# The start of a state-space kernel: normalize, transpose and split ahead of the branch, splits on GpSimd, gates ahead of the mixing matrix

## The reference, cut to what matters

```
xn  = layernorm(x)                       # x: 8 batches x 512 tokens x 512
xz  = xn @ W_in.T;  x_ssm, z = split(xz) # 1024 + 1024 columns
xc  = silu(causal_conv4(x_ssm) + conv_b)
p   = xc @ W_x.T                         # 16 B, 16 C, one dt
dt  = softplus(p[..., -1] + mean(dt_bias));  A = -exp(A_log)
h_t = exp(A dt_t) h_{t-1} + dt_t B_t x_t;  y_t = C_t . h_t
s   = ((y + D xc) * silu(z)) @ out_W.T
g   = silu(ffn_with_attention(xn))
out = x + s * g
```

## Time and profile before

| | |
|---|---|
| three runs | 2586.34 us median (2586.32 to 2586.46) |
| the profiled execution | 2587.55 us, its span 2585.4 us |
| PE busy | 2487.2 us, 96% of the span |
| DVE busy | 1382.6 us, 53% |
| ACT busy | 1059.4 us, 41% |
| POOL busy | 439.8 us, 17% |
| mean granted TensorE clock | 0.989 |
| first 110 us: PE busy | 70.12 us |
| 110 to 182 us: PE busy | 71.76 us |
| batch 1: last add into PFM (L1161) | 194.81 to 195.50 us |
| batch 1: turned(1, 0) on PE starts | 199.78 us |

### The profile page before, as it was taken

The page is one execution under the profiler, slowest core; times in us unless marked ns, Lnnn a source line. Parts: engine busy times, 40 slices in busy tenths (PEclk is TensorE's granted clock), DMA queues, the critical chain, the costliest instruction groups (busy, mean ns, idle before and its releaser), DMA issues.

```text
span 2585.4 us, 38397 instructions
## 1 busy us (share of the span) xinstructions
PE 2487.2 (96%) x14359; PEld 2002.0 (77%) x14359; DVE 1382.6 (53%) x2876; ACT 1059.4 (41%) x1764; POOL 439.8 (17%) x407
## 2 busy tenths in 40 slices
PE   5899999999999899999999899999999999999998
PEld 4678778778788677777777678888888788888887
DVE  6666667567565578888888852212213422222223
ACT  4444444444544367777777641111112211111111
POOL 0000000000000234444443610000000202222222
PEclk8999999999999999999999999999999999999999
DMA  4000000000003577666566411111113312222212
GB/s 140 17 17 17 33 17 17 33 1 33 17 1 103 162 213 207 188 183 185 155 183 184 153 58 49 49 49 49 49 49 110 135 41 97 96 98 95 97 66 82
DMA packets 106972, 228.12 MB, mean 88 GB/s; under 512 B 14976, under 2 KB 15488, under 8 KB 100624
## 3 DMA queue, kind: packets, MB, share of 16 engines
q1 hardware_dynamic: 106528, 225.34, 27.2%
q10 hardware_dynamic: 256, 0.26, 0.0%
HBM read 149.77 MB, written 75.50 MB: 87 GB/s over the span
## 4 chain that ended last, share of the span: by engine, by line
PE 86%; DVE 6%; ACT 3%; issue 3%; DMA 2%; SPq 0%; POOL 0%; DVEq 0%; POOLq 0%; ACTq 0%
PE PS L72 13%; PE PS L74 13%; PE PS L73 13%; PE PS L2122 4%; PE PS L2123 4%; PE PS L2124 4%; PE PS L1622 3%; PE PS L1641 3%; PE PS L1599 2%; PE PS L708 2%; PE PS L707 2%; PE PS L709 2%; PE PS L1601 2%; PE PS L1600 2%; PE PS L693 1%
## 5 line engine op out<-in xcount | busy, mean ns | idle before, releaser
L2191 DVE TENSOR_TENSOR SG<-SG,PS 128x512 f32<-128x512 f32 x124 | 85.2, 687 | 645.4 <-PE PS L74 643.5
L72 PE MATMUL PS<-FH,GU 128*128 128x512 f32 x992 | 387.4, 390 | 1.4 <-DVE DW L2182 1.4
L74 PE MATMUL PS<-FH,GU 128*128 128x512 f32 x992 | 388.3, 391 | 0.0
L73 PE MATMUL PS<-FL,GU 128*128 128x512 f32 x992 | 387.5, 391 | 0.0
L1807 DVE CUSTOM_DVE_ANT_0 PS<-PS,MK 128x512 f32<-128x512 f32 (+3 forms) x512 | 243.8, 504 | 95.2 <-PE PS L1622 94.0
L2161 ACT ACTIVATE SG<-PS 128x512 f32<-128x512 f32 x124 | 74.0, 597 | 467.3 <-PE PS L2098 467.3
L1744 ACT ACTIVATE PF<-PS 128x512 f32<-128x512 f32 (+1 forms) x384 | 199.6, 526 | 84.8 <-PE PS L1643 82.8
L2227 POOL TENSOR_SCALAR XN<-XT,MEAN,RSTD 128x512 f32<-128x512 f32 x32 | 69.5, 2171 | 943.6 <-DMA M<-m_scratch 943.6
L2164 ACT CAST GH<-SG 128x512 fp32r<-128x512 f32 x124 | 76.9, 620 | 351.7 <-DVE SG L2191 351.7
L72 PE MATMUL PS<-XH,WH 128*128 128x512 f32 x512 | 211.1, 412 | 9.9 <-DVE XL L977 9.9
L72 PEld LDWEIGHTS PS<-FH,GU 128*128 128x128 f32 x992 | 186.4, 188 | 42.5 <-issue 1.8
(11 more groups left out here) (296 smaller groups left out, 5306.1 us busy)
## 6 DMA issues: line engine op xcount, KB each, us to landing
qk_scratch<-QT SPq DMA_DIRECT2D x128, 256.0 KB, 4.6
QS<-qk_scratch SPq DMA_DIRECT2D x96, 256.0 KB, 4.0
KS<-qk_scratch SPq DMA_DIRECT2D x96, 256.0 KB, 3.9
FH<-rh_scratch SPq DMA_DIRECT2D x16, 1024.0 KB, 5.7
FL<-rl_scratch SPq DMA_DIRECT2D x16, 1024.0 KB, 7.9
XF<-in_x_dram SPq DMA_DIRECT2D x32, 256.0 KB, 3.8
s_scratch<-ZS SPq DMA_DIRECT2D x8, 1024.0 KB, 4.4
rh_scratch<-RH SPq DMA_DIRECT2D x8, 1024.0 KB, 9.6
```

What stands on the lines that cost most here:

```text
L72: pe.matmul(o, lh(k), xh(k), start=open_ and k == 0, stop=False, skip_group_check=True)
L73: pe.matmul(o, lh(k), xl(k), start=False, stop=False, skip_group_check=True)
L74: last = pe.matmul(o, ll(k), xh(k), start=False, stop=close and k == nk - 1, skip_group_check=True)
```

## The change

- The first code, ahead of the branch, takes over much of the start. DVE: after step 4 of fast_deviations it makes four constants (which waits for the loads of idn and UM, c_ld 32), normalizes the four tiles of XF, runs step 5, makes the other constants, then split_lo(0) and the four lowered, and last RMS. PE: the 16 transposes of normed. ACT: the exponential of A_log, split_hi(0), normed_hi, split_hi(1). Each engine branches only after that.
- split_lo(1), (2) and (3) and the two subtractions for OL go from DVE to POOL, at the head of its fast path, ahead of RC (L1201) of batch 0.
- out_hi(0) and out_hi(4) on ACT move into the conv loop, at d = 4 and d = 5.
- gate(0, 0) on PE moves ahead of rows(0, 6), into bank 2 (bank_g); it waits for s_cv 9.
- For all batches: gate(b, 2) stands ahead of decays, gate(b, 3) ahead of factors_turned, gate(b, 4) ahead of off_diagonal, and none between off_diagonal and gate(b, 5). On ACT gated(b, 2) stands ahead of the two exponentials, and the later ones follow.
- Counts of semaphores follow; the general path, not run here, waits for what the first code started.

```diff
@@ first_vector
-            for step in range(8):
+            for step in range(5):
                 fast_deviations(dve, 0, step)
+            block_constants(dve, 0)
+            for k in range(4):
+                fast_normalized(dve, 0, k)
+            fast_deviations(dve, 0, 5)
+            block_constants(dve, 1)
+            dve.wait_ge(c_ld, 32)
+            split_lo(dve, 0)
+            for k in range(4):
+                lowered(dve, 0, k)
+            fast_rms(dve, 0)
@@ first_tensor
+            pe.wait_ge(c_ld, 32)
+            for k in range(4):
+                normed(pe, 0, k)
@@
+        def bank_g(b, m):
+            return m % 2 if b or m else 2
@@
+        def block_constants(dve, part):
+            if part == 0:
+                dve.wait_ge(c_ld, 32)
...
@@ first_scalar
+            act.wait_ge(c_al, 32)
+            act.activation(AB_[:, :], AR[:, :], ACT.Exp).then_inc(s_ka, 1)
             act.wait_ge(c_dve, 5)
             split_hi(act, 0)
+            for k in range(4):
+                normed_hi(act, 0, k)
+            split_hi(act, 1)
@@ gate
                 if m == 0:
-                    pe.wait_ge(s_cv, 21 if b == 0 else 24 * b + 24)
+                    pe.wait_ge(s_cv, 9 if b == 0 else 24 * b + 24)
...
-                project(b, 8 + m, m % 2)
+                project(b, 8 + m, bank_g(b, m))
@@ spread
                 if b:
                     pe.wait_ge(s_oc, 4 * (b - 1) + 2)
+                else:
+                    pe.wait_ge(s_zc, 1)
@@ fast_tensor
+            gate(0, 0)
             rows(0, 6)
             rows(0, 7)
             for b in range(NB):
-                gate(b, 0)
+                if b:
+                    gate(b, 0)
                 rows_turned(b)
                 gate(b, 1)
                 spread(b)
+                gate(b, 2)
                 decays(b)
-                gate(b, 2)
+                gate(b, 3)
                 factors_turned(b)
-                gate(b, 3)
+                gate(b, 4)
                 off_diagonal(b)
-                gate(b, 4)
                 gate(b, 5)
@@ fast_scalar, the conv loop
+                if d in (4, 5):
+                    out_hi(4 * (d - 4))
@@ fast_scalar, the mixing stage
                 gated(b, 1)
+                gated(b, 2)
                 act.wait_ge(s_ag, 6 * b + 5)
...
-                gated(b, 2)
+                gated(b, 3)
@@ fast_vector
-            split_lo(1)
...
-                if d == 5:
-                    split_lo(2)
...
-                    split_lo(3)
...
-                    for i, k in enumerate((0, 4)):
-                        dve.wait_ge(s_oh, i + 1)
-                        dve.tensor_tensor(OL[:, k:k + 4, :], OS[:, k:k + 4, :], f32(OH[:, k:k + 4, :]), ALU.subtract).then_inc(s_ol, 1)
@@ fast_pool
+            for c in range(1, 4):
+                split_lo(pool, c)
+            for i, k in enumerate((0, 4)):
+                pool.wait_ge(s_oh, i + 1)
+                pool.tensor_tensor(OL[:, k:k + 4, :], OS[:, k:k + 4, :], f32(OH[:, k:k + 4, :]), ALU.subtract).then_inc(s_ol, 1)
```

More of the change, by code:

```diff
@@ L179, in fetched_ahead @@
             e.wait_ge(s_nm, 4)
+            e.wait_ge(c_dve, 17)
+            e.wait_ge(s_ka, 1)
+            e.wait_ge(s_tx, 4)
+            e.wait_ge(s_xh, 4)
+            e.wait_ge(s_xl, 4)
+            for k in range(2):
+                e.wait_ge(s_wh[k], 1)
+            e.wait_ge(s_wl[0], 1)
         def gen_sync(sp):
@@ L565, in fast_deviations @@
             if step == 6:
-                dve.wait_ge(s_pw, 2 * b + 2)
-                dve.tensor_tensor(RMS[:, c], VT[:, 2, :], RSTD[:, c], ALU.mult).then_inc(s_ln, 1)
+                fast_rms(dve, b)
             if step >= 6:
                 for k in (2 * step - 12, 2 * step - 11):
[L570 to L573, removed]
+                    fast_normalized(dve, b, k)
@@ new lines, in fast_rms, with fast_normalized, normed @@
+        def fast_rms(dve, b):
+            c = slice(4 * b, 4 * b + 4)
+            dve.wait_ge(s_pw, 2 * b + 2)
+            dve.tensor_tensor(RMS[:, c], VT[:, 2, :], RSTD[:, c], ALU.mult).then_inc(s_ln, 1)
+        def fast_normalized(dve, b, k):
+            n, X = 4 * b + k, XF[k][:, :]
+            dve.wait_ge(s_ln, 14 * b + 9)
+            dve.wait_ge(s_pw, 2 * b + 1)
+            dve.tensor_scalar(X, X, MEAN[:, n:n + 1], RSTD[:, n:n + 1], ALU.subtract, ALU.mult).then_inc(s_nm, 1)
+        def normed(pe, b, k):
+            bank = bank_x[k]
+            if b:
+                if k < 2:
+                    pe.wait_ge(s_g, 7 * b - 4)
+                elif k == 2:
+                    pe.wait_ge(s_ml, 4 * b - 3)
+                else:
+                    pe.wait_ge(s_nl, 8 * b - 7)
+            pe.wait_ge(s_nm, 4 * b + k + 1)
+            for d in range(4):
+                t = pe.transpose(PS[bank][:, 128 * d:128 * d + 128], XF[k][:, 128 * d:128 * d + 128], idn[:, :])
+            t.then_inc(s_tx, 1)
@@ new lines, in normed_hi, with lowered @@
+        def normed_hi(act, b, k):
+            bank = bank_x[k]
+            act.wait_ge(s_tx, 4 * b + k + 1)
+            if b:
+                act.wait_ge(s_pj, 16 * b)
+            act.copy(tokens(XH, k), PS[bank][:, :].rearrange("p (d t) -> p d t", d=4)).then_inc(s_xh, 1)
+        def lowered(dve, b, k):
+            bank = bank_x[k]
+            dve.wait_ge(s_xh, 4 * b + k + 1)
+            dve.tensor_tensor(tokens(XL, k), PS[bank][:, :].rearrange("p (d t) -> p d t", d=4), f32(tokens(XH, k)),
+                              ALU.subtract).then_inc(s_xl, 1)
@@ L887, in out_hi @@
                 act.copy(OH[:, k:k + 4, :], OS[:, k:k + 4, :]).then_inc(s_oh, 1)
-            act.activation(AB_[:, :], AR[:, :], ACT.Exp).then_inc(s_ka, 1)
-            for k in range(4):
-                normed_hi(0, k)
-            split_hi(act, 1)
             act.wait_ge(s_w, 80)
@@ L910, in fast_scalar @@
                     out(b - 1, 1)
-                if b == 0:
-                    out_hi(0)
                 gated(b, 0)
@@ L936, in fast_scalar @@
                 act.copy(CBT[:, :], PS[5][0:80, :]).then_inc(s_e2, 1)
-                gated(b, 3)
+                gated(b, 4)
                 act.wait_ge(s_l2, b + 1)
@@ L942, in fast_scalar @@
                     act.copy(MH[:, J, 128:128 + n], PS[bank][:, at:at + n]).then_inc(s_mh, 1)
-                gated(b, 4)
                 act.wait_ge(s_g, 7 * b + 7)
@@ L1173, in fast_vector @@
                     for k in range(4):
-                        lowered(b + 1, k)
+                        lowered(dve, b + 1, k)
                 mixed(b, 0)
```

104 lines of the change are left out of this document (37 added, 67 removed).

## The result

The changed kernel takes **2565.78 us** (median of four runs, 2564.88 to 2567.64); the kernel before took 2586.4 (2586.32 to 2588.29) beside it. The ratio is 0.9921, 95% interval 0.9907 to 0.9935: 20.6 us faster, 0.8%. The forecast was 2571.9, in a range of 2561 to 2579. The profiled execution took 2565.04 us, 2563.2 of it span; against the profile of before that is 22.5 us less. PE is busy for 81.1 of the first 110 us (70.1 before).

What follows compares the result with a forecast made beforehand. PE, busy for nearly the whole span, was taken as the bound, so only its gaps and low clock could be won. -6.4 + 6.6 - 10.0 - 4.6 = -14.4 us from 2586.34 gave 2571.9 us, range 2561 to 2579.

Steps and rivals of the forecast that it cites:

- Rival 1: Conv loop: conv_lo(3) gets in ahead of POOL's split, rows_turned -0.5 rather than +6.6; 2564.8 us, chance 0.27.
- Front: Start up to the first projection: it begins at 20.0 us in place of 26.45, -6.4 us.
- Conv loop: Batch 0's convolution: POOL's splits hold up conv_lo, rows_turned at 73.8 rather than 67.23, +6.6 us.
- the lock: Conv loop: DVE's two-input conv_lo waits for POOL's whole instruction, up to 4.8 us per split.
- POOL starts at 49.3, ahead of conv_lo(3): Conv loop: POOL's split starts some 0.3 us ahead and holds until 54.1; conv_lo(3) ends at 54.8, later holds follow.
- 1.5 us for a falling clock: Conv loop: PE gaps of about 4 us lower the granted clock; 1.5 us added, of 0 to 3.
- Rival 2: Conv loop: POOL doesn't stop DVE, rows_turned at 63.5, -3.7; 2561.6 us, chance 0.08.
- Rival 3: Conv loop: POOL becomes the bound at 9.7 us a split, 2589.2 us; chance 0.06 for no change, 0.03 for slower.
- Rival 4: Front: DVE's branch waits for POOL's first split, DVE back 4.6 us after needed; 2576.5 us, chance 0.11.
- Mixing stage: Batch 0, rows_turned to first mix: subtractions ahead of BF go, one gate fewer behind it; -10.0 us.
- bound of -8.5: Mixing stage of batch 0: smallest gain, if the remaining wait for BF, about 1.8 us, keeps the clock low.
- Batches 1 to 7: Later batches: gate(b, 2) covers the 0.65 us wait of decays for DTB in each, -4.6 us.

Runs made afterwards that it cites:

- late output weights: Changed kernel, but the eight loads of the output weights are issued only when the first projection is done; 2563.97 us, ratio 0.9916.
- third split early: Changed kernel, but split_hi(3) on ACT one turn of the conv loop earlier, so GpSimd starts its third split ahead of conv_lo(0, 3); 2566.36 us, ratio 0.9924.
- clearing in front of conv_lo(3): Changed kernel plus a clearing of BF1 on VectorE in front of conv_lo(3), meant to let GpSimd's third split start first; 2566.66 us, ratio 0.9922.
- start behind the branch: Changed kernel, but normalizing last, transposes, splits and constants stand behind the branch again, as before; 2568.31 us, ratio 0.9941.
- old gates: Changed kernel, but batches 1 to 7 have the earlier kernel's order of gates and decays, batch 0 left as changed; 2572.8 us, ratio 0.9951.
- late normalization: Changed kernel, but VectorE's normalization of batch 1's rows moves from in front of BF to behind turned_lo(0, 0); 2562.65 us, ratio 0.9908.
- both late: Changed kernel with both the late normalization and the late output weights; 2562.66 us, ratio 0.9905.
- in pieces: Changed kernel, but each of GpSimd's five subtractions of 128x2048 cut into four of 128x512; 2566.24 us, ratio 0.9921.
- one half of OL moved away: Late normalization, second half of input weights loaded later, only OL's first subtraction behind split_lo(1), the second still behind split_lo(3); 2562.13 us, ratio 0.9909.
- with both: Late normalization, second half of input weights loaded later, both OL subtractions on GpSimd behind split_lo(1), ahead of split_lo(2); 2568.93 us, ratio 0.9925.

## Why the prediction was right, and where it wasn't

The range and the direction held; the sum was 6.1 us too cautious. Between the two profiles 22.2 us of span were gained where it has 14.4: the front gave 2.8 less than its term, the conv loop 6.7 more, the mixing stage 0.3 and the batches 1.4 more, and 2.2 came behind the last mix, where the forecast has nothing. Rival 1 gives a time closer to the measured one, 2564.8. Its term for the loop is nearly right; that its sum is too is in part luck, since it shares the front's error and lacks the last 2.2 us.

**Front, -6.4 against -3.6.** The links that decide the first projection came close to what was written: XF at 10.13, transposes at 10.82 (10.7), 5.4 us to get on behind the branch (3.96 to 5.9), first projection at 19.88 (20.0). The term was counted to that point and taken to last. It didn't: a second stall cost 2.44 within the block. The run with the late output weights shows that it hangs on the transfers, since there it is gone. The rest of the 2.8 is of the same block, most of which ran at a granted clock of 0.50. PE had no such stall in the kernel before, but DVE had one, within its first 6 us behind the branch, a sign that one stall was not the whole price:

```profile
25.02 1.29 DVE L977 TENSOR_TENSOR XL<-PS,XH 128x512 fp32r<-128x512 f32 x2 [1.84 <-issue]
```

**Conv loop, +6.6 against -0.1: the step that failed.** The price (4.56 to 4.90 us a split, forecast 4.8) and the lock were right. What failed is the chain "POOL starts at 49.3, ahead of conv_lo(3)", then each further hold added to the last. The margin of that race was 0.3 us, and what leads up to it came out shorter by more: the split of block 2 took 4.61 us, not 4.8, conv_lo(2) ended 0.55 behind it, not 0.7, and conv_lo(3) was due 2.15 behind that, not 2.31. In the profile conv_lo(3) got in, 0.26 us ahead, and the calls of d = 4, 5 and 6 were held by 0.6, 2.0 and 2.2 us. That is rival 1's case, with holds of the size it names (1 to 2 us), and -0.1 is close to its -0.5. The Trainium skill has a price too (GPSIMD Engine Reference, "3.1 Elementwise — side-by-side cycle accounting": 4497 ns for an add of 2048 columns), and the subtractions of this case that started ahead of VectorE, 4.54 to 4.63 us, agree with it. In the forecast's own chain 4.5 us instead of 4.8 takes the whole margin away; it would have spoken for rival 1.

That the order of this pair is what makes the 7 us between the forecast and rival 1 isn't shown: the run that held conv_lo(3) by 2.2 us ended the loop at the same time, and the forecast's own case, a hold of nearly the whole split, was not run. The forecast also had OL's second half wait for ACT until 61.3, in the times of before; it ran straight behind the first.

What the runs do show is that the loop's end hangs on POOL's own queue. In the eight profiles in which both of OL's halves are done whole behind split_lo(3) and gate(0, 0) stands ahead of rows(0, 6), the end of its last subtraction and the start of rows_turned are 2.6 us apart. The last column is the loop, from the first rows to rows_turned:

| kernel | POOL's last subtraction ends | rows_turned | between | loop |
|---|---|---|---|---|
| after | 60.93 | 63.54 | 2.61 | 27.97 |
| third split early | 61.00 | 63.59 | 2.59 | 27.99 |
| clearing in front of conv_lo(3) | 61.75 | 64.36 | 2.61 | 28.39 |
| late output weights | 57.48 | 60.11 | 2.63 | 27.98 |
| start behind the branch | 62.66 | 65.27 | 2.61 | 27.97 |
| old gates | 62.14 | 64.75 | 2.61 | 27.98 |
| late normalization | 61.47 | 64.09 | 2.62 | 27.97 |
| both late | 57.76 | 60.38 | 2.62 | 27.98 |

Six of them have the same loop to 0.01 us and only start it at another time, so their equal distance says little. What tells is the two that change something within the loop (the third split early leaves POOL's last pair and the end where they were, the clearing moves both by 0.4) and the versions without the last hold: the loop takes 25.15 us with the splits on VectorE, 25.30 in pieces, 25.71 with one half of OL moved away, 26.05 with both. In after's profile the last two calls of conv_lo wait for the last subtraction (58.61, 3.47 us for both; 1.3 of it work), then come the last rows and PFM. With one half moved away they take 2.12 in all and the loop is 2.3 us shorter; its end comes 2.8 sooner because the constants' transposes came 3.2 sooner too, of which a longer wait for the constants took 2.6 back.

That the loop came out even against before has two sides. GpSimd's holds cost it 2.8 us (27.97 against 25.15, where VectorE even has one split to do within the loop), and gate(0, 0) ahead of rows(0, 6) gains 4.3 up to rows_turned with the holds there (67.81 against 63.54), 1.4 of it by the clock that stays up. What the gate gains without the holds was not run. The forecast's 1.5 us for a falling clock didn't come in after's profile; behind rows_turned it came in three others (clearing, old gates, late normalization), as 1.4 to 1.6.

**Rival 2** (POOL doesn't stop DVE) is out: conv_lo took up to 2.87 us instead of 0.68. **Rival 3** is out with 4.6 to 4.9 a split. **Rival 4** had its mechanism right and its consequence wrong. The small operation, the last one of DVE ahead of its branch, was held in after's profile:

```profile
18.37 3.18 DVE L598 TENSOR_TENSOR RMS<-VT,RSTD 128x4 f32<-128x4 f32 x1
```

It takes 0.15 us alone. It ended at 21.55, with POOL's split (16.97 to 21.53). But DVE's next task, the constants' copies, waited for PE until 28.58, so nothing was late.

**Mixing stage, -10.0 against -10.3.** The wait for BF came out at 1.77 (1.8), and two OL subtractions less on VectorE did what was said. The parts agree as well: rows_turned to CK gave 0.8 (forecast 0.4), CK to BF 4.4 (4.4), BF to the first mix 5.2 (4.7 and 0.5). The run with the splits on VectorE shows the reverse: 6.2 again. The clock stayed up behind the 1.8 us gap, as the -10.0 assumes; in the profiles of three other versions (in pieces, late output weights, start behind the branch) it fell there, which is the forecast's bound of -8.5.

**Batches 1 to 7, -4.6 against -6.0.** The mechanism was right, the size small: 0.86 us a batch between the profiles, 0.89 in the profile of the run with the old gates, where the row of the wait has 0.65. The difference of 0.2 a batch is not in any wait that the profile shows. It lies beside the wait that is gone (above); what it is stays open. The 1.0 by that run's medians says too much: its profile also has 2.8 us more than after's at a low clock, around the constants and behind rows_turned.

## What to carry to other kernels

Work moved to GpSimd is paid twice: VectorE's operations with two SBUF inputs, and some with one, wait for the rest of each instruction, and the last of them can set when the loop ends. So put GpSimd's long instructions where VectorE reads PSUM or is idle, and look at when its queue runs dry rather than at who wins one race. A gain ahead of a branch or a fetch has to be read off at a mark well behind it, since the next fetch may take it back. When a race of 0.3 us decides a term of several, the sum is only as good as the price to a tenth. And price a removed wait by the marks either side of it, not by its row: a gate of 2.75 us in place of a gap gave 4.2, since the clock no longer fell behind it, and seven waits of 0.65 gave 6.

## What the runs showed of the hardware

- One GpSimd subtraction with two inputs, 128x2048 to fp32r, takes 4.54 to 4.63 us where it starts ahead of VectorE, 4.9 to 5.3 where a two-input call of VectorE was under way. The same columns in four pieces took 5.5 us, waits for VectorE included.
- The lock takes small operations of VectorE too, and not only those with two inputs: a tensor_scalar on 16 columns, SBUF to SBUF, took 4.48 us, a 4-column tensor_tensor 3.18. It does not take all: beside a split of GpSimd (24.04 to 28.63 us, start behind the branch) a tensor_reduce with one SBUF input took 0.37 us, and the taps of the convolution, with one operand in PSUM, took the same 2.3 us for three beside a split (39.81 us, after) as without. GpSimd waits as well where VectorE is first: 5.34 us instead of 4.61. The Trainium skill names, beside two SBUF inputs, operations in a two-port mode as takers of the lock (SBUF — State Buffer, "SBUF: two separate sides"). The tensor_scalar's row fits that if it ran in that mode, which no run here shows.
- A stall that is read as a fetch of instructions depends on the transfers beside it: 2.44 us at a DMA share of 1.06, none at 0.13. Another near the end of the attention, in a stretch at 252 GB/s, is 1.5 to 1.6 us in three profiles (before's is one), 0.5 to 1.2 in others, and has no row in after's.
- Behind gaps of 1.6 to 1.8 us the granted clock stayed at 1.00 in some profiles and fell in others, with matmuls of 0.63 rather than 0.39 us: 1.4 to 1.6 us each time. Each version has one profile, so whether this also makes the difference between runs of one kernel isn't shown.
- The granted clock of a window can miss a slow stretch: from 20 to 22 us it is 0.50 in after and 1.00 in the run with gate(0, 0) moved back, and in both the matmuls of 512 columns take 0.63 us.
